# An LSTM recurrence with attention on one Trainium2 core: the softmax's division moved behind the mixing

## The reference, cut to what matters

```python
def step(carry, x_t):
    h0, c0, h1, c1, a = carry
    xin = jnp.concatenate([x_t, a], axis=-1)
    h0, c0 = _lstm_cell(xin, h0, c0, Wi0, Wh0, bi0, bh0)
    h1, c1 = _lstm_cell(h0, h1, c1, Wi1, Wh1, bi1, bh1)
    q = h1 @ Wq.T
    attn = jax.nn.softmax(jnp.einsum('bh,bsh->bs', q, context), axis=-1)
    mixed = jnp.einsum('bs,bsh->bh', attn, context)
    a2 = jnp.tanh(jnp.concatenate([mixed, h1], axis=-1) @ Wo.T + bo)
    return ((h0, c0, h1, c1, a2), a2)
```

## Time and profile before

| | us |
|---|---|
| median of 3 runs | 8344.06 (8343.58 to 8344.1) |
| the profiled execution, its own time | 8346.82 |
| its span, first to last instruction | 8345.0 |
| busy in the span: TensorE (matmul) | 6831.2 (82%) |
| busy: TensorE (weight load) | 5806.1 (70%) |
| busy: VectorE | 4214.3 (51%) |
| busy: ScalarE | 3382.3 (41%) |
| busy: GpSimd | 332.6 (4%) |
| mean granted TensorE clock, share of full | 0.979 |

### The profile page before, as it was taken

One profiled execution on the slowest core, in us unless ns is written; L12 is line 12 of the kernel. 1 busy time (PEld: TensorE's weight loads), 2 busy tenths in 40 slices (PEclk: granted clock), 3 DMA queues, 4 the chain that ended last, 5 costly groups with the idle time before them and its releaser, 6 DMA issues. The chain is left out here.

```text
span 8345.0 us, 815594 instructions
## 1 busy us (share of the span) xinstructions
PE 6831.2 (82%) x380504; PEld 5806.1 (70%) x380505; DVE 4214.3 (51%) x21197; ACT 3382.3 (41%) x17078; POOL 332.6 (4%) x342
## 2 busy tenths in 40 slices
PE   7888888888888888888888888888888888766769
PEld 5777777777777777777777777777777777644546
DVE  5555454455454454554544544454454544575822
ACT  4444444444444444444444444444444444432422
POOL 0000000000000000000000000000000000021622
PEclk8999999999999999999999999999999999988879
DMA  2000000000000000000000000000000000000143
GB/s 86 5 0 0 0 0 0 0 0 0 0 0 0 0 0 0 0 0 0 0 0 0 0 0 0 0 0 0 0 0 0 0 0 0 0 6 18 65 165 107
DMA packets 58666, 94.52 MB, mean 11 GB/s; under 512 B 14202, under 2 KB 45952, under 8 KB 57472
## 3 DMA queue, kind: packets, MB, share of 16 engines
q1 hardware_dynamic: 53248, 81.38, 3.0%
q0 software_dynamic: 5376, 12.63, 0.4%
HBM read 76.08 MB, written 20.00 MB: 12 GB/s over the span
## 5 line engine op out<-in xcount | busy, mean ns | idle before, releaser
L307 PE MATMUL scan_sums<-rec_wh,scan_hT 128*4 128x64 f32 x131008 | 2394.2, 219 | 2.6 <-issue 2.5
L428 DVE STREAM_TRANSPOSE scan_sums<-scan_sums 128x64 f32<-128x64 f32 x6144 | 1546.6, 266 | 1137.2 <-PE scan_sums L307 1136.7
L307 PEld LDWEIGHTS scan_sums<-rec_wh,scan_hT 128*4 128x4 f32 x131008 | 1991.4, 89 | 3.4 <-issue 3.4
L307 PE MATMUL scan_sums<-rec_wa,scan_aT 128*4 128x64 f32 (+1 forms) x65536 | 1104.7, 219 | 381.8 <-ACT scan_aT L389 381.8
L307 PEld LDWEIGHTS scan_sums<-rec_wa,scan_aT 128*4 128x4 f32 (+1 forms) x65536 | 915.6, 88 | 570.6 <-ACT scan_aT L389 570.6
L307 PE MATMUL scan_sums<-rec_wx,scan_xT 128*4 128x64 f32 (+1 forms) x65536 | 1291.6, 219 | 7.4 <-issue 6.5
L307 PE MATMUL scan_sums<-rec_wi,scan_hT 128*4 128x64 f32 (+1 forms) x65536 | 1103.1, 219 | 142.5 <-issue 2.5
L307 PEld LDWEIGHTS scan_sums<-rec_wi,scan_hT 128*4 128x4 f32 (+1 forms) x65536 | 914.3, 88 | 331.1 <-DVE scan_hT L478 328.5
L307 PEld LDWEIGHTS scan_sums<-rec_wx,scan_xT 128*4 128x4 f32 (+1 forms) x65536 | 1023.7, 89 | 8.1 <-issue 7.1
L373 ACT ACTIVATE scan_tanh_f<-scan_sums 128x8 f32<-128x8 f32 x2048 | 364.0, 178 | 1188.0 <-DVE scan_sums L428 1188.0
L368 ACT ACTIVATE scan_sums<-rec_bias 128x192 f32<-128x192 f32 x2050 | 686.8, 335 | 302.8 <-PE scan_sums L347 5.5
(11 more groups left out here) (254 smaller groups left out, 6166.6 us busy)
## 6 DMA issues: line engine op xcount, KB each, us to landing
experts_bias<-in_b SPq DMA_DIRECT2D x40, 640.0 KB, 4.4
moe_w<-in_w SPq DMA_DIRECT2D x16, 1024.0 KB, 12.3
slots_x<-route_blank SPq DMA_DIRECT2D x40, 129.0 KB, 2.5
experts_x<-slots_x SPq DMA_DIRECT2D x40, 129.0 KB
w_xres<-in_x_steps SPq DMA_DIRECT2D x8, 512.0 KB, 11.1
w_xres<-in_x SPq DMA_DIRECT2D x4, 1024.0 KB
x_rows<-w_xres SPq DMA_DIRECT2D x4, 1024.0 KB, 11.3
rec_wh<-in_wh SPq DMA_DIRECT2D x2, 1024.0 KB, 14.8
```

The costliest lines, as they stand in the source:

```text
L307: last = nc.tensor.matmul(sums[layer][BANK[g]][32 * j:32 * j + ROWS[g], 0:64], state[:, k, FIRST[g]:FIRST[g] + ROWS[g]], weight[:, k, j, 6 ...
L428: nc.vector.transpose(turned[l][g], sums[l][g][:, 0:64]).then_inc(gates_turned[l][g], 1)
```

## The change

The exponentials are no longer divided by their sum ahead of the product with `vp`. The product takes them as they are, into columns 192 to 255 of the bank `scores`. VectorE copies `woh`'s result out of `a_sum` (`from_h`). Four matmuls with one moving column take the four sums, which ScalarE now writes to SBUF (`total`), from partitions 0, 33, 66 and 99 and lay all four on each partition group (column 256 of `a_sum`); VectorE takes the reciprocal there, multiplies the mixed rows with it and adds `from_h`, and turns the result into `a_sum`'s bank. On TensorE gate g of `wx` moves from ahead of the mixing to behind it. The `exp` takes 64 columns in place of 65.

```diff
-        total = scores[:, 128:129]
+        mixed, spread_total = scores[:, 192:256], a_sum[:, 256:257]
...
+        from_h, a_natural = m.sbuf("from_h", [P, 64]), m.sbuf("a_natural", [P, 64])
+        neg_max, total, inv = m.sbuf("neg_max", [P, 1]), m.sbuf("total", [P, 1]), m.sbuf("inv", [P, 1])
+        own_rows = w["ident"][:, 0:100:33]
...
-                    head_product(scores, state_of(hT[1]), w["kp"], True, True).then_inc(scores_done, 1)
-                    head_product(a_sum, state_of(hT[1]), w["woh"], True, False)
+                    head_product(scores, state_of(hT[1]), w["kp"]).then_inc(scores_done, 1)
+                    head_product(a_sum, state_of(hT[1]), w["woh"]).then_inc(h_summed, 1)
                     if not last:
                         product(0, hT[0], w["wh0"], (GATE_O,))
                         pe.wait_ge(x_ready, n + 1)
-                        product(0, xT[(s + 1) % 2], w["wx"], (GATE_F, GATE_I, GATE_G))
-                    pe.wait_ge(probs_ready, n)
-                    head_product(a_sum, pT[:], w["vp"], False, True).then_inc(a_summed, 1)
+                        product(0, xT[(s + 1) % 2], w["wx"], (GATE_F, GATE_I))
+                    pe.wait_ge(h_kept, n)
+                    pe.wait_ge(exps_done, n)
+                    for j in range(4):
+                        spread = nc.tensor.matmul(spread_total[32 * j:32 * j + B, :], own_rows, total[:], start=True, stop=True,
+                                                  skip_group_check=True)
+                    spread.then_inc(total_spread, 1)
+                    pe.wait_ge(exps_turned, n)
+                    head_product(mixed, expsT[:, :, 0:B], w["vp"]).then_inc(a_terms, 1)
                     if not last:
-                        product(0, xT[(s + 1) % 2], w["wx"], (GATE_O,))
+                        product(0, xT[(s + 1) % 2], w["wx"], (GATE_G, GATE_O))
...
-                    nc.scalar.activation(exps[:], scores[:, 0:S + 1], ACT.Exp, bias=neg_max[:],
-                                         accum_out=total).then_inc(exps_done, 1)
+                    nc.scalar.activation(exps[:], scores[:, 0:S], ACT.Exp, bias=neg_max[:],
+                                         accum_out=total[:]).then_inc(exps_done, 1)
...
+                    dve.wait_ge(h_summed, n)
+                    nc.vector.tensor_scalar(from_h[:], a_sum[:, 0:64], 1.0, None, ALU.mult).then_inc(h_kept, 1)
                     dve.wait_ge(exps_done, n)
-                    nc.vector.reciprocal(inv[:], total).then_inc(inv_done, 1)
-
-                    nc.vector.transpose(expsT[:].rearrange("p k s -> p (k s)"), exps[:, 0:S]).then_inc(p_turned, 1)
-                    dve.wait_ge(inv_done, n)
-                    nc.vector.transpose(invT[:], inv[:].broadcast_to([P, 32])).then_inc(p_turned, 1)
-                    dve.wait_ge(p_turned, 2 * n)
-                    nc.vector.tensor_tensor(pT[:], expsT[:, :, 0:B], invT[:, None, 0:B].broadcast_to([P, 2, B]),
-                                            ALU.mult).then_inc(probs_ready, 1)
-                    dve.wait_ge(a_summed, n)
-                    nc.vector.transpose(a_sumT, a_sum[:, 0:64]).then_inc(a_turned, 1)
+                    nc.vector.transpose(expsT[:].rearrange("p k s -> p (k s)"), exps[:]).then_inc(exps_turned, 1)
+
+                    dve.wait_ge(total_spread, n)
+                    nc.vector.reciprocal(inv[:], spread_total).then_inc(a_terms, 1)
+                    dve.wait_ge(a_terms, 2 * n)
+                    nc.vector.scalar_tensor_tensor(a_natural[:], mixed, inv[:], from_h[:], ALU.mult, ALU.add).then_inc(a_scaled, 1)
+                    dve.wait_ge(a_scaled, n)
+                    nc.vector.transpose(a_sumT, a_natural[:]).then_inc(a_turned, 1)
```

More of the change, by code:

```diff
@@ L271, in scan @@
         state_of = lambda tile: tile[:, :, B:2 * B]
-        exps, expsT, invT = m.sbuf("exps", [P, S + 1]), m.sbuf("expsT", [P, 2, 32]), m.sbuf("invT", [P, 32])
-        pT = m.sbuf("pT", [P, 2, B])
-        neg_max, inv = m.sbuf("neg_max", [P, 1]), m.sbuf("inv", [P, 1])
+        exps, expsT = m.sbuf("exps", [P, S]), m.sbuf("expsT", [P, 2, 32])
+        from_h, a_natural = m.sbuf("from_h", [P, 64]), m.sbuf("a_natural", [P, 64])
+        neg_max, total, inv = m.sbuf("neg_max", [P, 1]), m.sbuf("total", [P, 1]), m.sbuf("inv", [P, 1])
+        own_rows = w["ident"][:, 0:100:33]
         gates_summed = [[m.sem(f"summed_{g}{l}") for g in ("f", "ig", "o")] for l in range(2)]
@@ L278, in scan @@
                                                                for n in ("f_tanh", "c_terms", "c_done", "c_kept", "h_factors", "h_ready"))
-        (a_ready, x_ready, scores_done, max_done, exps_done, p_turned, probs_ready, a_summed, inv_done, a_turned, a_kept, zeroed) = (
-            m.sem(n) for n in ("a_ready", "x_ready", "scores_done", "max_done", "exps_done", "p_turned", "probs_ready", "a_summed",
-                               "inv_done", "a_turned", "a_kept", "zeroed"))
+        (a_ready, x_ready, scores_done, max_done, exps_done, exps_turned, h_summed, h_kept, total_spread, a_terms, a_scaled, a_turned,
+         a_kept, zeroed) = (m.sem(n) for n in (
+             "a_ready", "x_ready", "scores_done", "max_done", "exps_done", "exps_turned", "h_summed", "h_kept", "total_spread",
+             "a_terms", "a_scaled", "a_turned", "a_kept", "zeroed"))
         opened = m.sem("opened")
@@ L312, in product, with head_product @@
                             last.then_inc(done[BANK[g]], 1)
-                def head_product(bank, state, weight, start, stop):
+                def head_product(bank, state, weight):
                     for k in range(2):
@@ L317, in head_product @@
                             last = nc.tensor.matmul(bank[32 * j:32 * j + B, 0:64], state[:, k, :], weight[:, k, j, :],
-                                                    start=start and k == 0, stop=stop and k == 1, skip_group_check=True)
+                                                    start=k == 0, stop=k == 1, skip_group_check=True)
                     return last
@@ L423, in _ @@
                 dve.wait_ge(a_ready, 1)
-                nc.vector.memset(pT[:], 0.0).then_inc(zeroed, 1)
+                nc.vector.memset(mixed, 0.0)
+                nc.vector.memset(spread_total, 1.0).then_inc(zeroed, 1)
                 def turn(l, g, n):
```

## The result

The changed kernel takes 8314.92 us (median of 7 runs, 8308.81 to 8317.23) against 8344.18 us (7 runs, 8343.58 to 8345.57): a ratio of 0.9963, 95% interval 0.9954 to 0.9973. It is faster, by 29 us, where 89 were forecast, and lies above the range of 8160 to 8308.

What follows compares the result with a forecast made beforehand. A chain through the engines, 7.04 us a step, was taken to bound the kernel; 0.393 - 0.282 - 0.035 + (0.266 - 0.245) - 0.010 = 0.087 us, times 1024 = 89 us, forecasting 8255 us, range 8160 to 8308.

Steps and rivals of the forecast that it cites:

- Taken off the path: Between reciprocal's start and pT's end: 0.618 us replaced by one 0.225 us transpose, so the mixing starts 0.393 us earlier.
- The scale-and-add: VectorE instruction added behind the mixing: 0.282 us a step, with 0.223 as its cheap bound.
- The wait on itself: VectorE's wait between scale-and-add and last turn: 0.035 us added, bounds 0.03 and 0.05.
- The last turn: VectorE's closing transpose, now SBUF to PSUM: 0.245 us in place of 0.266, bounds 0.225 and 0.266.
- The readout: ScalarE's sum written to SBUF instead of PSUM: 0.010 us more, bounds 0 and 0.016, from tanh rows.
- Costed at nothing: Work beside the path: from_h copy, spread and reciprocal (0.05 to 0.16 us to spare), gates g and o behind the mixing.
- The extra waits on TensorE: One or two more waits, held to cost nothing because TensorE is idle where they stand.
- A: On TensorE, the mixing's weight loads wait for the spread's matmuls, 0.15 us late: slower, about 8409 us; chance 0.05.
- B: One-column spread matmuls pipeline badly, so the scale-and-add waits for the reciprocal: slower, about 8685 us; chance 0.03.
- C: VectorE's two instructions and their wait take 0.65 us instead of 0.56, eating the gain: 8305 to 8344; chance 0.10.
- dear end: Unknown costs at their highest bounds (282, 0.05, 266, 0.016): gain of 0.045 us a step, 46 us, giving 8298.

Runs made afterwards that it cites:

- b1: The kernel before, with only the exp's sum read out to SBUF instead of PSUM; 8364.41 us, ratio 1.0032.
- a7: a2 with one wait on TensorE ahead of the mixing in place of three; 8312.89 us, ratio 0.9958.
- a2: The changed kernel without the four spread matmuls and the reciprocal, a constant 0.05 as scale, so no division by the totals; 8398.56 us, ratio 1.0074.
- a5: The changed kernel with gate g of wx back ahead of the mixing; 8314.80 us, ratio 0.9971.

## Why the prediction was wrong in size

The direction, the place of the gain and the place of the cost were right, so the mechanism held. What failed are three terms of the sum, each too cheap: the transpose in the first term (by 0.020 us), the readout (0.017) and the last turn (0.015), together 0.052 of the 0.087 forecast. The misses all pointed the same way and none offset another. Going through the steps:

- *Taken off the path, 0.393 us.* This term was mis-sized. It took the transpose's 0.225 us from a row in which it ran behind the reciprocal, though the prediction itself made it the first instruction after the wait. There it takes 245 ns, as the run with the two lines exchanged shows in the kernel before too. The term is 0.373 (0.618 - 0.245), and it had been given no bounds at all, so the range did not know of it.
- *The scale-and-add, 0.282.* Measured 0.283. The wait on itself, 0.035: measured 0.035.
- *The last turn, 0.245.* Measured 0.260. The step that failed is the splitting of the difference between 266 and 225: 20 of the 41 ns were again first or not first, and of the rest 15 are the PSUM write and 6 the read. The 21 ns that were given to the read came from comparing two reciprocals of different stages; b1 has 5 ns there (169 against 164). The bound of 266 held. The Trainium skill (VectorE: DVE Perf Modes, the TRN2 errata's table), from whose cycles the read would be worth an estimated 65 ns, is not borne out for this transpose: 266 against 260.
- *The readout, 0.010.* Its own row goes from 166 to 193, 27 ns, outside the bounds of 0 to 16, which came from a tanh. The sum needs 17 ns more; b1 shows the 27 ns on the chain, less the 5 of its reciprocal.
- *Costed at nothing.* from_h ended at 5.91 in the timeline, 0.25 us ahead of the transpose; the spread and the reciprocal are beside the mixing, which a7 without them shows (7.005 against 7.008 us a step); gates g and o end well before aT. All three right. The extra waits on TensorE, costed at nothing since it is idle there, were right only by luck: they stand ahead of the spread, which is off the chain. Ahead of the mixing the same two cost 0.09 us a step (a2 against a7), as much as the whole forecast gain. Moving gate g does bring the spread forward, but only by 0.04 us (a5), and nothing hangs on it.
- *Rivals.* A (the mixing waits behind the spread) did not happen: the mixing starts 0.055 us after the transpose's end, at 6.46, while the spread's matmuls still run to 6.48. The rule that spoke for it (the Trainium skill, TensorE: Matmul & The Clock Gate, Part 3) does not fit the changed kernel's rows either: wx's loads start at 6.63 while the mixing's matmuls run from 6.46 to 6.87. B did not happen, the reciprocal is done 0.21 us early, more than the 0.05 to 0.16 forecast. C gave the right interval, 8305 to 8344, for the wrong reason: the two VectorE instructions and their wait take 0.578 us, not 0.65; the rest of the missing gain is ahead of the mixing.
- *The range.* Its dear end was 46 us of gain. With the transpose's 20 and the readout's further 11 ns (27 in place of its bound of 16) it would have been 14, and the range would have held the 29.

## What to carry to other kernels

On a chain of small instructions, take a duration only from a row in which the instruction stands as it will: first after a wait or behind a running one, and with the same memories at both ends; here this was 15 to 40 ns of some 200 each, and three such errors took more than half of the forecast gain. Count the waits ahead of the instruction that ends a leg, and wait only for the last of several events where it covers the others. And ask what a wait is really released by: here the transpose needs the exponentials but gets the semaphore of the sum's readout, 0.09 us later.

## What had not been expected of the hardware

- Taking four matmuls and a reciprocal out made the program slower than the changed kernel (ratio 1.0074 against 0.9963, step time 7.096 against 7.008), because two more waits then stood ahead of the matmul at the end of a leg; without them the ratio was 0.9958 and the step time 7.005. Two more waits on TensorE ahead of one matmul cost 0.09 us a step here, though both had long been fulfilled.
- The same VectorE instruction shows 20 to 40 ns less behind a running one than after idle time or a wait: the 64-column transpose 225 against 246, the 32-column one 180 against 211, the reciprocal 129 against 169.
- The readout of ScalarE's accumulator takes 166 ns to PSUM and 193 to SBUF, 27 ns more, where a tanh shows 16. VectorE's transpose of the exponentials waits for it, 0.09 us longer than for the exp alone.
- A per-partition scalar adds 58 ns to a 64-column scale-and-add (225 to 283), and 64 from PSUM (289).
